# Sixty-four node rows at a time: the aggregation products of a graph stage, split over the two halves of the matmul array

## What is computed

```python
# layer 0: U = eigenvectors (64 x 64) of a Laplacian of adj
agg = jnp.einsum('mn,bnd->bmd', U.T, features)          # over the 64 nodes
h   = jax.nn.relu(agg @ W1 + b1)                        # 256 -> 128
out = h @ W2 + b2                                       # 128 -> 256
x   = layernorm(x + jnp.einsum('nm,bmd->bnd', U, out))
# layer 1, before its LSTM
h = jax.nn.relu(jnp.einsum('ts,bsh->bth', adj, x @ Wg0 + bg0))
h = jax.nn.relu(jnp.einsum('ts,bsh->bth', adj, h @ Wg1 + bg1))
```

## Time and profile before

| | |
|---|---|
| median of three runs | 2471.44 us (2471.21 to 2472.2) |
| the profiled execution's own time | 2466.92 us |
| its span in the profile | 2465.1 us |
| TensorE busy in the span | 1802.4 us (73%) |
| stretch of this stage | about 585 to 900 us from the span's start |

### The profile page before, as it was taken

How to read it: one execution, slowest core, us unless ns; L and a number is a source line. 1 busy time by engine, 2 the same in 40 slices (tenths; PEclk the granted TensorE clock), 3 DMA queues, 4 the chain that set the end, 5 groups by cost and what they waited for, 6 DMA issues and landing times. The chain is left out here.

```text
span 2465.1 us, 33696 instructions
## 1 busy us (share of the span) xinstructions
PE 1802.4 (73%) x9259; PEld 1473.0 (60%) x9259; DVE 1502.3 (61%) x5909; ACT 860.8 (35%) x1752; POOL 670.2 (27%) x1058
## 2 busy tenths in 40 slices
PE   2444000004999959999999999999995998768885
PEld 1333000002777638888889999988884886655553
DVE  4999999882555535644444444443444777657875
ACT  1332111000333316633333343332232666445563
POOL 0010444200111106643333333422220114423332
PEclk9999999999999989999999999999997999989898
DMA  6000000000000000000000000000003212200111
GB/s 150 1 1 1 1 1 1 1 0 24 26 34 26 34 30 13 17 13 9 9 13 9 0 9 9 1 0 0 0 0 146 85 60 69 80 9 26 34 34 35
DMA packets 44517, 62.27 MB, mean 25 GB/s; under 512 B 13952, under 2 KB 33152, under 8 KB 44288
## 3 DMA queue, kind: packets, MB, share of 16 engines
q1 hardware_dynamic: 32992, 61.17, 7.2%
q10 hardware_dynamic: 11424, 0.05, 0.3%
HBM read 36.04 MB, written 25.17 MB: 25 GB/s over the span
## 5 line engine op out<-in xcount | busy, mean ns | idle before, releaser
L1814 PE MATMUL ps<-l_nodes_in,l_weights 128*128 128x512 f32 (+1 forms) x3024 | 619.5, 365 | 23.0 <-remote 20.7
L1814 PEld LDWEIGHTS ps<-l_nodes_in,l_weights 128*128 128x128 f32 x3024 | 533.0, 188 | 104.3 <-issue 26.5
L1880 ACT ACTIVATE l_gates<-ps,biases 128x512 f32<-128x512 f32 (+1 forms) x504 | 288.8, 635 | 506.2 <-remote 491.7
L1814 PE MATMUL ps<-l_state,l_weights 128*128 128x512 f32 (+1 forms) x1728 | 341.2, 356 | 0.0
L1814 PEld LDWEIGHTS ps<-l_state,l_weights 128*128 128x128 f32 x1728 | 298.5, 188 | 37.4
L1925 DVE TENSOR_TENSOR l_gates<-l_gates 128x512 f32<-128x512 f32 (+1 forms) x72 | 48.5, 674 | 346.0 <-ACT l_gates L1880 346.0
L1773 POOL CAST l_nodes_in<-big 128x512 fp32r (+3 forms) x142 | 102.0, 746 | 576.5 <-remote 531.8
L1776 POOL TENSOR_TENSOR l_nodes_in<-big,l_nodes_in 128x512 fp32r<-128x512 f32 (+1 forms) x142 | 201.0, 1436 | 5.7
L953 PE MATMUL ps<-sw_one,tab 64*1 64x1 f32 x4 | 0.4, 160 | 226.0 <-DVE sw_one L623 217.0
L953 PEld LDWEIGHTS ps<-sw_one,tab 64*1 64x1 f32 x4 | 0.2, 77 | 226.3 <-DVE sw_one L623 217.2
L1923 DVE TENSOR_TENSOR l_cell<-l_gates 128x512 f32<-128x512 f32 (+1 forms) x72 | 54.3, 754 | 107.6 <-ACT l_gates L1880 107.0
(11 more groups left out here) (517 smaller groups left out, 3588.8 us busy)
## 6 DMA issues: line engine op xcount, KB each, us to landing
x<-in_x SPq DMA_DIRECT2D x4, 2048.0 KB, 18.4
residual<-s_x SPq DMA_DIRECT2D x16, 512.0 KB, 2.6
x_late<-residual SPq DMA_DIRECT2D x16, 512.0 KB, 10.8
normed<-j_x SPq DMA_DIRECT2D x16, 512.0 KB, 2.6
x_late<-normed SPq DMA_DIRECT2D x16, 512.0 KB, 3.2
out<-a_y SPq DMA_DIRECT2D x16, 512.0 KB, 2.9
l_raw<-in_L_gnn_W SPq DMA_DIRECT2D x16, 256.0 KB, 2.7
l_raw<-in_L_gnn_W SPq DMA_DIRECT2D x4, 512.0 KB, 3.9
```

Source lines behind the costliest of these rows:

```text
L1814: return pe.matmul(ps[:, 4 * j + gate, 0:n], w[:, w_part, at:at + 128].bitcast(F32R), src[:, part, k, 0:n].bitcast(F32R), start=start, sto ...
L1880: act.activation(gates[:, j, gate, 0:n], ps[:, 4 * j + gate, 0:n], ACT.Tanh if gate == G else ACT.Sigmoid, bias=bias[:, gate * KD + j:gate ...
```

## The change

Each product of 128 rows by 128 moving columns becomes two of 64 rows by 64 moving columns: the first takes partitions 0 to 63 of the activations and the upper block of the matrix, the second partitions 64 to 127 and the lower block. The zeros are no longer multiplied. The stationary operand is 64 rows x 128 features each time. The two halves write to different banks of the pair (`out[:, half, ...]`), each bank filled in the order of chunk, tile. So the columns of the result stand in PSUM in another order, and the three copies of ScalarE read them through `by_half` and write them through `in_order`, in pieces of 64 columns. No wait, semaphore or buffer changes.

```diff
+    def by_half(pair):
+        return pair.rearrange("p h (a n) -> p a h n", n=NODES)
+
+    def in_order(agg):
+        return agg[:, :, :].rearrange("p k n -> p (k n)").rearrange("p (a h n) -> p a h n", h=2, n=NODES)
+
...
                 for k in range(KD):
                     for i in range(TILES):
-                        mm = pe.matmul(out[:, k, i * TILE:(i + 1) * TILE], src[:, i, k * 128:(k + 1) * 128], mix[:, :],
-                                       start=True, stop=True)
+                        for half in range(2):
+                            rows, at = slice(NODES * half, NODES * (half + 1)), (k * TILES + i) * NODES
+                            mm = pe.matmul(out[:, half, at:at + NODES], src[rows, i, k * 128:(k + 1) * 128],
+                                           mix[rows, rows], start=True, stop=True)
                 mm.then_inc(ready, 1)
...
             def first():
-                move(A0, agg0[:, :, :], a0_ready, a0_moved)
+                move(by_half(A0), in_order(agg0), a0_ready, a0_moved)
...
             def second():
-                move(A1, agg1[:, :, :], a1_ready, a1_moved)
+                move(by_half(A1), in_order(agg1), a1_ready, a1_moved)
...
             def third():
-                move(B, agg1[:, :, :], b_ready, b_moved)
+                move(by_half(B), in_order(agg1), b_ready, b_moved)
```

## The result

The changed kernel takes 2482.41 us (median of 5 runs, 2481.26 to 2486.87) where the kernel before takes 2471.44 us (5 runs, 2469.26 to 2474.68). The ratio is 1.0048, with a 95% interval from 1.0034 to 1.0063: slower by 11.0 us. The profiled execution took 2482.41 us, its span is 2480.6 us.

A forecast was written before the change was run, and what follows sets the result against it. TensorE, busy 213.4 of 220 us in the loop, was taken as the bound. 5.2 us in 14 steps plus 0.9 at the edges gave +6.1 on 2471.4, so 2477.5 us; range 2469 to 2557.

The forecast's parts named there:

- the likeliest case: Aggregations: both halves load at once, and the array empties at each change of shape; 2477.5 us, chance 0.60.
- The load sets the pace, whatever its rows: Aggregations: within one half, a load of 128 stationary columns takes 0.107 us, also with half the rows.
- Halves at once, 0.112 a pair: Aggregations: the two row halves work at once, 0.112 us a pair, so 16 pairs take 1.79 us as before.
- The rival of serial loads: Aggregations: loads of the two halves go one after the other, +83 us, 2554 us; chance 0.17.
- Emptying the array, +0.37 a step: Around a0 and a2 in the loop: TensorE drains at both shape changes, +0.37 us a step, 5.2 us in 14 steps.
- a1's share lies in the gap: Ahead of conv1 in the loop: TensorE's 0.55 us idle gap absorbs a1's +0.37 us, shrinking to 0.18; no cost.
- Copies at nothing: ScalarE's copies in 16 pieces of 64 columns: taken as zero extra time, 2.4 us at most.
- Edges, 0.9 us: First and last steps of the stage: shape changes of aggregations not hidden by copies add 0.9 us.
- the clock falls: Loop steps: if half-filled products weighed as idle, each step could have 3.4 us at 1.2 GHz; 2501 us, chance 0.03.

The follow-up runs named there:

- the second time: The changed kernel run once more without edits: 2486.49 us beside 2471.32 for the kernel before, ratio 1.0063.
- the kernel with the halves apart: Changed kernel with each aggregation's 16 upper-half products first, then its 16 lower-half ones: 2607.08 us beside 2471.32 for the kernel before, ratio 1.0549.
- the two kernels that split a part: Changed kernel with only a1 split: 2474.02 us, ratio 1.0007; with only a0 and a2 split: 2483.05 us, ratio 1.0044, both against the kernel before.
- Four quarters: Changed kernel with each product also split over its features, 64 rows x 64 stationary columns: 2468.78 us beside 2470.74 for the kernel before, ratio 0.9989.

## Why the prediction came out as it did

The direction was right, and 2482.4 lies in the range, but the likeliest case gave 2477.5: +6.1 where +11.0 was measured, and +15.2 the second time, both outside that case's own range of 2474 to 2481. That the full range holds the result is luck in part, for its upper end was set by a case that didn't come true.

*The load sets the pace, whatever its rows* held. One half alone goes at 0.111 us a load in the kernel with the halves apart. The Trainium skill, TensorE: Matmul & The Clock Gate, section LDWEIGHTS (loading the stationary operand), says that the columns of a load count and its rows don't; the trace agrees, 0.188 us for 64 rows and 0.192 for 128. The prediction had this from L1276, which it took to run at 1.2 GHz by its durations. The clock row reads 1.00 there (30.90 to 32.60), which the prediction doesn't say; as at the head of the stage, the durations were the better guide.

*Halves at once, 0.112 a pair* held: 2 x 0.054 = 0.108 by the loads, 2 x (2.00 - 0.272)/31 = 0.111 by the matmuls. The scores' column halves were a good guide for row halves. The rival of serial loads, whose price set the upper end of the range, did not happen.

*Emptying the array, +0.37 a step* was 0.34, so 4.8 us in the 14 steps for 5.2. back0's last columns are through at 710.14 (708.42 + 1.88 - 0.592 + 0.43), and a0's first load starts at 710.23, 0.09 us later. *a1's share lies in the gap* held, shown by the two kernels that split a part, and by 0.68 against 0.34 once the gap was gone. *Copies at nothing* held, 1024 ns for 1023.

*Edges, 0.9 us* is the term that was mis-sized. They cost 6.3 us in the first trace (2.0 ahead, 4.3 behind), more in the second, and 9.0 us in the kernel with halves at the ends alone. The mechanism stood among the rivals, "the clock falls", but was priced for every loop step (24 us) and dismissed by a stretch that held scores and was full otherwise. In the loop it indeed stayed at 1.00 (615 to 875 us): the aggregations lie between whole products, with 0.21 us of idle time a step. At the ends they lie between waits of 1 to 3 us, and the prediction priced no clock there.

What stays open is what exactly tips the clock at the ends, since waits and half-filled products come together there. With whole products and much the same waits one to three products were slow in each trace, so the waits alone do little; with split ones five to ten were. In the kernel with the halves apart the clock fell almost without waits, but there only one half works at a time. Whether the halves must write different banks was not tried.

## What to carry to other kernels

Here, splitting a product by rows halved its matmul but not its weight load; where the two were equal, nothing was gained until the stationary columns were split too. Each change of the array's shape costs about 0.17 us here, so group the products of one shape, and look for a wait that covers the rest. Price a change that fills less of the array also where TensorE waits, at the ends of a pipelined loop, because the clock may fall there though it doesn't in the loop; and before making an engine faster, read which chain the next wait hangs on.

## What the hardware did that I had not expected

- The granted clock fell with TensorE busy 349 of 350 us, to 0.82 on average, in the kernel that fills one half of the array at a time; with halves by turns and the same products it stayed at 1.00 in the loop.
- By the names in the trace, with the halves apart, matmuls of a2 (711.84) started before the last matmuls of a0 (711.94), which stand ahead of them in the program; all 32 of each are in the trace. By the program's order the former are on the upper half and the latter on the lower, so the two halves took their products side by side, each in its own order.
- Four quarters took 64 loads and 64 matmuls in 1.05 us, 0.016 us a product with a load of 64 columns, against 0.111 for one with a load of 128 columns in one half of the array.
- The clock row of the profile read 1.00 over stretches whose products took twice as long (hidden at 590.01 in the changed kernel, the first a0 before the change with 3.66 us for 1.95), both ahead of the first fall that it shows.
